# First-layer attention: the softmax division is done quad by quad between later units, with sums and reciprocals laid out by tokens

## What is computed

```python
q, k, v = xn @ Wq.T + bq, xn @ Wk.T + bk, xn @ Wv.T + bv     # 16 heads of 8
p = softmax(q @ k.T / sqrt(8))                                # 512 x 512 per head
out = ((p @ v) * head_mask) @ Wo.T + bo
```

## Time and profile before

| | us |
|---|---|
| median of 3 runs | 4028.96 (4026.98 to 4035.01) |
| the profiled execution | 4031.42 |
| its span, first to last instruction | 4030.1 |
| TensorE busy (share of the span) | 3097.7 (77%) |
| VectorE busy | 2581.5 (64%) |
| ScalarE busy | 2028.4 (50%) |
| GpSimd busy | 1557.2 (39%) |
| mean granted TensorE clock | 0.84 of full |
| first scores of attending in the first-layer attention, to its end | 118.2 to 672.95 |

### The profile page before, as it was taken

One profiled execution on the slowest core, in us unless ns is written; L12 is line 12 of the kernel. 1 busy time (PEld: TensorE's weight loads), 2 busy tenths in 40 slices (PEclk: granted clock), 3 DMA queues, 4 the chain that ended last, 5 costly groups with the idle time before them and its releaser, 6 DMA issues.

```text
span 4030.1 us, 40714 instructions
## 1 busy us (share of the span) xinstructions
PE 3097.7 (77%) x14760; PEld 1359.4 (34%) x14850; DVE 2581.5 (64%) x2891; ACT 2028.4 (50%) x3628; POOL 1557.2 (39%) x938
## 2 busy tenths in 40 slices
PE   5788877975567777777775879777687888888876
PEld 2111212341222222232322644322234554554544
DVE  4676662439998888888787334577625655555563
ACT  1454453134456766766664211576435565555654
POOL 2211100113457667666657002244414443443432
PEclk7788897986778888887777979888698998999998
DMA  3221200021111221121111001001000000000000
GB/s 86 41 33 30 45 3 0 0 75 39 26 35 37 42 51 32 40 49 36 32 34 45 1 0 64 21 21 32 11 0 19 19 19 10 19 19 10 19 10 31
DMA packets 79733, 114.60 MB, mean 28 GB/s; under 512 B 16270, under 2 KB 49422, under 8 KB 78106
## 3 DMA queue, kind: packets, MB, share of 16 engines
q1 hardware_dynamic: 68268, 103.33, 10.7%
q0 software_dynamic: 11264, 8.66, 1.6%
HBM read 37.96 MB, written 17.33 MB: 14 GB/s over the span
## 4 chain that ended last, share of the span: by engine, by line
PE 49%; DVE 21%; ACT 16%; issue 7%; POOL 3%; DMA 2%; SPq 1%; POOLq 0%; DVEq 0%; ACTq 0%
DVE layer_mamba_state L1340 7%; PE psum L1112 3%; DVE psum L1328 3%; PE psum L2460 3%; ACT layer_mamba_decay L1266 3%; PE psum L1189 3%; PE psum L2491 3%; PE psum L779 2%; ACT layer_exps L792 2%; PE psum L236 2%; PE psum L248 2%; PE psum L2154 2%; PE psum L905 2%; PE psum L242 2%; PE psum L2544 2%
## 5 line engine op out<-in xcount | busy, mean ns | idle before, releaser
L1369 POOL TENSOR_TENSOR layer_mamba_state<-layer_mamba_state,layer_mamba_c 128x1024 f32<-128x1024 f32 x320 | 781.0, 2450 | 591.3 <-DVE layer_mamba_state L1340 585.1
L1340 DVE TENSOR_TENSOR_SCAN layer_mamba_state<-layer_mamba_decay,psum 128x1024 f32<-128x1024 f32 x320 | 731.4, 2286 | 43.7 <-ACT layer_mamba_decay L1266 11.5
L1189 PE MATMUL psum<-layer_mamba_state,two_to_one 128*64 128x512 f32 x1280 | 442.9, 784 | 124.1 <-DVE layer_mamba_x L1357 80.9
L1266 ACT ACTIVATE layer_mamba_decay<-layer_mamba_delta_wide,layer_weights 128x511 f32<-128x511 f32 x640 | 415.7, 711 | 76.1 <-DMA layer_mamba_delta_wide<-layer_mamba_delta 39.5
L1328 DVE TENSOR_TENSOR psum<-psum,layer_mamba_u_wide 128x1024 f32<-128x1024 f32 x320 | 393.3, 1229 | 62.0 <-PE psum L1147 26.0
L720 DVE TENSOR_REDUCE layer_peak<-psum 128x2 f32<-128x1024 f32 x256 | 306.6, 1218 | 112.7 <-PE psum L691 108.6
L792 ACT ACTIVATE layer_exps<-psum 128x1024 f32<-128x1024 f32 x256 | 250.8, 1029 | 222.6 <-PE psum L759 222.6
L2857 POOL TENSOR_TENSOR layer_p<-layer_p,layer_stats 128x512 f32<-128x512 f32 x128 | 133.2, 1041 | 299.0 <-DVE layer_stats L2780 298.8
L2651 ACT ACTIVATE layer_p<-psum,layer_stats 128x128 f32<-128x128 f32 x512 | 181.5, 369 | 130.1 <-DVE layer_stats L2773 129.6
L2844 POOL TENSOR_TENSOR layer_qk<-layer_qk,layer_v_between 128x1024 f32<-128x1024 f32 x64 | 150.5, 2351 | 216.1 <-DVE layer_v_between L2744 214.3
L1147 PE MATMUL psum<-layer_mamba_bc,layer_mamba_pick 96*64 96x512 bf16 x768 | 164.2, 455 | 87.5 <-DVE psum L1328 63.7
(11 more groups left out here) (349 smaller groups left out, 6185.8 us busy)
## 6 DMA issues: line engine op xcount, KB each, us to landing
layer_mamba_delta_wide<-layer_mamba_delta SPq DMA_DIRECT2D x160, 128.0 KB, 2.4
layer_mamba_u_wide<-layer_mamba_work SPq DMA_DIRECT2D x160, 128.0 KB, 2.4
layer_v_between<-layer_v SPq DMA_DIRECT2D x16, 512.0 KB, 4.3
qk_dram<-layer_qk_parts SPq DMA_DIRECT2D x16, 384.0 KB, 3.0
layer_q_rows<-qk_dram SPq DMA_DIRECT2D x96, 64.0 KB
layer_k_rows<-qk_dram SPq DMA_DIRECT2D x96, 64.0 KB
layer_v_between<-layer_v SPq DMA_DIRECT2D x16, 384.0 KB, 5.6
layer_weights<-weights_dram SPq DMA_DIRECT2D x1, 4147.0 KB, 12.2
```

The lines of the kernel that those rows point to most:

```text
L1189: e = pe.matmul(c.psum[j * HALF:(j + 1) * HALF, self.sum_banks[h], :], c.two_to_one[:, :], self.state[i % len(self.state)][:, j, :], start ...
L1266: e = act.activation(decay[:, j, 1:SEQ], self.delta_wide[h][:, j, 1:SEQ], ACT.Exp, scale=rates[:, rate:rate + 1])
L1340: dve.tensor_tensor_scan(state, decay, self.fill.rearrange("p j t -> p (j t)"), 0.0, ALU.mult, ALU.add).then_inc(self.scanned, 1)
L1369: pool.tensor_tensor(state, state, self.both(self.c_wide[turn % self.C_BUFFERS][:, :]), ALU.mult).then_inc(self.multiplied, 1)
```

## The change

The sums are made per quad. For each block of 128 tokens the quad's tile is the weight operand and 4 columns of `sum_rows` move, so that sums come out by tokens: 128 rows by 4 columns, for four blocks 128x16 in bank 7. The reciprocal is taken there, 128x16, into `inverse`. To spread it over the quad's rows, a column of `inverse`, broadcast to 32 columns, is the weight operand and the identity moves: 16 products of 128 columns, into four groups of 32 rows by four blocks. Scaling and output product are as before.

The steps of `divide(b)` now have written-out times 32b + 10.6, 12.6 (quad 0: sums, spread), 18.6, 20.6 (quad 1), 28.6, 30.6 (quad 2), 34.6, 36.6 (quad 3) and 38.6 (output), for VectorE 0.6 and for ScalarE 0.9 later. The steps of `project` have 0.3 (wq), 3.6 (wk) and 8.8 (values) from 32(b-2), where they had 0.3, 2.3 and 6.3; SP's stores are at 1.3 and 4.6 and its row loads at 5.6 and 6.6, where they were at 1.3, 3.3, 4.3 and 5.3. The first sequence's projection is moved ahead by two units.

```diff
+    PROJECT_AT = (0.3, 1.3, 3.6, 4.6, 5.6, 6.6, 8.8, 9.8)
+    DIVIDE_AT = (10.6, 12.6, 18.6, 20.6, 28.6, 30.6, 34.6, 36.6, 38.6)
...
-        self.sums = buf("sums", [HEADS0, SEQ])
+        self.inverse = buf("inverse", [P, 4 * BLOCKS])
...
-        play(self.run(self.act_project, self.act_maxima, self.act_attend, self.act_divide))
-        play(self.run(self.dve_project, self.dve_maxima, self.dve_attend, self.dve_divide))
+        play(self.run(self.act_project, self.act_maxima, self.act_attend, self.act_divide, 0.9))
+        play(self.run(self.dve_project, self.dve_maxima, self.dve_attend, self.dve_divide, 0.6))
...
         for b in range(SEQS):
-            runs += [paced(divide(b), UNITS0 * (b + 1) + 1), paced(attend(b), UNITS0 * b + 0.1),
-                     paced(maxima(b), UNITS0 * (b - 1) - self.LEAD + 0.2),
-                     paced(project(b), (opening - 8, opening)[b] if b < 2 else UNITS0 * (b - 2) + 0.3)]
+            at = UNITS0 * (b - 2) if b > 1 else opening - 10 * (1 - b)
+            runs += [timed(project(b), [at + t for t in self.PROJECT_AT]), paced(maxima(b), UNITS0 * (b - 1) - self.LEAD + 0.2),
+                     paced(attend(b), UNITS0 * b + 0.1), timed(divide(b), [UNITS0 * b + t + after for t in self.DIVIDE_AT])]
...
     def pe_divide(self, b):
-        hold.wait_ge(self.heads_kept, QUADS0 * (b + 1))
-        c.wait_bank(7)
         for g in range(QUADS0):
-            m = pe.matmul(c.psum[0:HEADS0, 7, :], w["sum_rows"][:, g * HEADS0:(g + 1) * HEADS0], self.heads[g][:, :],
-                          start=g == 0, stop=g == QUADS0 - 1)
-        m.then_inc(self.sums_made, 1)
-        c.bank_read[7] = self.sums_inverted, b + 1
-        yield
-        for g in range(QUADS0):
-            hold.wait_ge(self.sums_inverted, b + 1)
+            n, first = QUADS0 * b + g + 1, g * HEADS0 + 4 * g
+            hold.wait_ge(self.heads_kept, n)
             c.wait_bank(7)
-            pe.matmul(bank, w["head_rows"][0:HEADS0, g * P:(g + 1) * P], self.sums[:, :], start=True, stop=True).then_inc(
-                self.sums_spread, 1)
-            c.bank_read[7] = self.heads_normed, QUADS0 * b + g + 1
+            for k in range(BLOCKS):
+                m = pe.matmul(bank[:, 4 * k:4 * k + 4], self.heads[g][:, k * P:(k + 1) * P], w["sum_rows"][:, first:first + 4],
+                              start=True, stop=True)
+            m.then_inc(self.sums_made, 1)
+            c.bank_read[7] = self.sums_inverted, n
+            yield
+            hold.wait_ge(self.sums_inverted, n)
+            c.wait_bank(7)
+            for k in range(BLOCKS):
+                for j in range(4):
+                    m = pe.matmul(c.psum[32 * j:32 * j + 32, 7, k * P:(k + 1) * P],
+                                  self.inverse[:, 4 * k + j:4 * k + j + 1].broadcast_to([P, 32]), c.ident[:, :],
+                                  start=True, stop=True)
+            m.then_inc(self.sums_spread, 1)
+            c.bank_read[7] = self.heads_normed, n
             yield
...
     def dve_divide(self, b):
-        hold.wait_ge(self.sums_made, b + 1)
-        hold.wait_ge(self.sums_spread, QUADS0 * b)
-        dve.reciprocal(self.sums[:, :], c.psum[0:HEADS0, 7, :]).then_inc(self.sums_inverted, 1)
-        yield
-        hold.wait_ge(self.out_made, b)
         for g in range(QUADS0):
-            hold.wait_ge(self.sums_spread, QUADS0 * b + g + 1)
+            n = QUADS0 * b + g + 1
+            hold.wait_ge(self.sums_made, n)
+            hold.wait_ge(self.sums_spread, n - 1)
+            dve.reciprocal(self.inverse[:, :], c.psum[:, 7, 0:4 * BLOCKS]).then_inc(self.sums_inverted, 1)
+            yield
+            hold.wait_ge(self.out_made, b)
+            hold.wait_ge(self.sums_spread, n)
```

More of the change, by code:

```diff
@@ L567, in nothing, with run @@
         return blank(0)
-    def run(self, project, maxima, attend, divide):
+    def run(self, project, maxima, attend, divide, after=0.0):
         runs, opening = [], -UNITS0 - self.LEAD
         for b in range(SEQS):
-            runs += [paced(divide(b), UNITS0 * (b + 1) + 1), paced(attend(b), UNITS0 * b + 0.1),
-                     paced(maxima(b), UNITS0 * (b - 1) - self.LEAD + 0.2),
-                     paced(project(b), (opening - 8, opening)[b] if b < 2 else UNITS0 * (b - 2) + 0.3)]
+            at = UNITS0 * (b - 2) if b > 1 else opening - 10 * (1 - b)
+            runs += [timed(project(b), [at + t for t in self.PROJECT_AT]), paced(maxima(b), UNITS0 * (b - 1) - self.LEAD + 0.2),
+                     paced(attend(b), UNITS0 * b + 0.1), timed(divide(b), [UNITS0 * b + t + after for t in self.DIVIDE_AT])]
         return merged(*runs)
@@ L836, in pe_divide @@
         c.bank_read[7] = self.attn_made, b + 1
-        yield
     def act_divide(self, b):
         c, act, hold = self.c, self.c.act, self.c.act_hold
-        yield from blank(1 + QUADS0)
+        yield from blank(2 * QUADS0)
         hold.wait_ge(self.out_made, b + 1)
         act.activation(self.out[:, b, :], c.psum[:, 7, :], ACT.Identity, bias=self.w["bo"]).then_inc(self.attn_made, 1)
-        yield
     def dve_divide(self, b):
         c, dve, hold = self.c, self.c.dve, self.c.dve_hold
-        hold.wait_ge(self.sums_made, b + 1)
-        hold.wait_ge(self.sums_spread, QUADS0 * b)
-        dve.reciprocal(self.sums[:, :], c.psum[0:HEADS0, 7, :]).then_inc(self.sums_inverted, 1)
-        yield
-        hold.wait_ge(self.out_made, b)
-        for g in range(QUADS0):
-            hold.wait_ge(self.sums_spread, QUADS0 * b + g + 1)
+        for g in range(QUADS0):
+            n = QUADS0 * b + g + 1
[5 more added lines that the diff above has]
+            hold.wait_ge(self.sums_spread, n)
             dve.scalar_tensor_tensor(self.normed[g][:, :], self.heads[g][:, :], self.w["mask_rows"][:, g:g + 1],
@@ L2911, in layer0_pieces @@
     sum_rows = np.zeros((P, QUADS0, HEADS0), np.float32)
-    head_rows = np.zeros((HEADS0, QUADS0, P), np.float32)
     for head in range(HEADS0):
@@ L2915, in layer0_pieces @@
         sum_rows[32 * j + DIM0, g, head] = 1.0
-        head_rows[head, g, 32 * j:32 * j + 32] = 1.0
     return {
@@ L2922, in layer0_pieces @@
         "mask_rows": np.repeat(i["L0_attn_head_mask"].reshape(QUADS0, 4), 32, axis=1).T,
-        "sum_rows": sum_rows.reshape(P, -1), "head_rows": head_rows.reshape(HEADS0, -1),
+        "sum_rows": sum_rows.reshape(P, -1),
     }, {
```

## The result

The changed kernel takes 3912.47 us (median of 4 runs, 3907.57 to 3920.47) against 4031.11 (4 runs, 4026.98 to 4035.01): ratio 0.9712, 95% interval 0.9698 to 0.9726. It is 119 us faster; 124 were forecast. The profiled execution took 3907.57, that of before 4031.42.

A forecast was written before the change was run, and what follows sets the result against it. Around the division no engine is full; they wait for each other at clock 0.69. Five periods of 71.6 us become 55.2 (-82); with +4, -12.6, -17, -16.2 that is -124, to 3908, or 3905 on the median's footing; range 3872 to 3950.

The forecast's parts named there:

- A boundary without low clock: Between sequences: with the division's boundary gone, turns and load take 46.1 us at full clock, before inserts.
- the low clock stays: Rival, chance 0.12: 5 us at half clock stay at each boundary, +15, 3920 us.
- Slack of 0.83 us in an even place: Behind a turn's first peak scores, 0.83 us of an insert is hidden; behind the second, the odd place, nothing.
- wk: Projection product at 3.6, an odd place: 1.15 us plus 0.35 for the last quad's reciprocal, together 1.5.
- The quads' sums: Sums take 1.2 us; shown: quad 3 0.35, quad 1 0.9, quad 0 1.55, the latter two behind their copy.
- The first two turns: Start of a period: wq shows 0.3 us and quad 3's sums at 2.6 show 0.35.
- The spread: Spreading a quad's inverses, 32 records: 1.2 us, near the weighing, of which 0.35 shows; three times, 1.05.
- the rival of the weight loads: Chance 0.12: loads in the open make a spread 0.9 us longer in 25 places, +23, 3928 us.
- VectorE's queue: Rival, chance 0.13: reciprocal and scaling ahead of the odd reduction hold TensorE's scores; period 62 us, total 3947.
- First sequence: Gains nothing, takes in quads 0 and 1 and the worse place of wk: +4.0 us.
- The eighth: Last sequence, ScalarE paces: 30.8 us of steps plus 2.5, 1.9 and 1.8 make 37.0, against 54.01.
- The tail: After the eighth, the last quad's division alone: 10 us against 26.25, output product 3.7 to 5 by the clock.

The follow-up runs named there:

- the last version: Changed kernel with the output product split into four quads' parts, every bank 7 product two units from the next, wk at 2.3: 3894.11 us, ratio 0.9666.
- the one with 16 columns inverted: Changed kernel's times with sums along the free dimension, the 4x512 reciprocal cut to its first 16 columns: 3920.2 us.
- the head by head order: Changed kernel with each spread's 16 products ordered so that four in a row go to the same group of 32 output rows: 3947.67 us.
- the 3.33 us reciprocal: Changed kernel's order, but sums and reciprocals along the free dimension, a reciprocal of 4x512 per quad: 4044.28 us, ratio 1.0036 to the kernel before.
- the layout alone: Kernel before with sums and reciprocals by tokens, all 16 heads at once at the boundary, in the old order: 3981.54 us, ratio 0.9875.

## Why the prediction was right

The forecast was 3905, the result 3912.5, inside the range and nearest to the case forecast. The stage gained 127.0 where the sum had 124, but part of this closeness is errors that cancel: the five periods, which I priced at 82 us, gave 86.8, and the other stretches 40 instead of 42. The changed kernel's profile is also the fastest of its four runs, 5 us below their median. By its steps:

- **A boundary without low clock.** Right, and the main thing. The five periods have clock 1.00. The rival "the low clock stays" is wrong for this kernel, but it was nearer than I thought: of the other kernels with short reciprocals, only the last version and the one with 16 columns inverted keep 1.00 in all five.
- **Slack of 0.83 us in an even place.** Right: spread 0.25 (forecast 0.35), values 0.35 (0.55), output 2.88 (2.9). Doubling the spread showed that it is used up.
- **wk** showed 1.08, not 1.5: the odd place has no cover, as said, but TensorE never waited for the reciprocal, only the load of its weights did. VectorE had done it at 227.85, 0.05 before wk.
- **The quads' sums.** Quad 0's wait for the copy is 0.66, with 0.96 shown (1.55), quad 1's, at 255.45, 0.38 with 0.69 shown (0.9). I had put a second copy's length, 0.7, for the value additions. They run from 240.54 to 241.41 and push back the reduction that the copy at 242.46 stands behind; against quad 1 this costs 0.28, not 0.7.
- **The first two turns**, wq and quad 3's sums, were too cheap at 0.65. The inserts above sum to 6.7 (three spreads among them), and 54.25 less 46.1 is 8.15, so 1.4 is left for them. The row at 226.03 names a part: the scores wait 0.94 for an exponential, where an undisturbed turn has 0.69, and this exponential stands in ScalarE's queue behind wq's bias step of 0.69, which I had costed at nothing. That is some 0.3 of the 0.8 that were missing. For the rest I have only an argument: no weighing stands in the first turn of a sequence, so an insert there finds less to hide behind than the 0.83 of a full turn.
- **The spread** took 1.01, where 1.2 was forecast. That it is near the weighing and not near single records was the choice that mattered most, and the head by head order shows how near the other side was: the rival of the weight loads gave 2.1, a mere change of loop order 2.39. (That rival's 0.13 us for a load pass doesn't follow from 0.16 for two; at 0.08 it would have stood at some 3920 instead of 3928.)
- **VectorE's queue.** The rival did not happen here: in the third sequence VectorE still idles 8.6 us before its 32 reductions, with 45.08 us busy (45.4 forecast). But with the 3.33 us reciprocal a chain through VectorE's queue does form, and costs more than the rival's 62: 74.3 to 75.9.
- **First sequence.** +4.0 forecast, +0.2 measured. The forecast was 3.8 too high: I added the inserts and took the clock as unchanged, but it was 0.90 before and is 0.97 after. By these two numbers that is some 3 of the 3.8 us, an estimate. Nothing shows that the change did it: the last version above has 0.91 there. So this term is as much luck as working.
- **The eighth**, 41.5 instead of 37.0, is the largest error. From the first exponential to the last, ScalarE is busy 31.6 us and idles 8.4 between its 33 steps; 0.4 ahead of them and the last weighing, 1.1 more, I had left out. I had 30.8 and 6.2. The output product alone holds up ScalarE for 2.93, not 1.9, since the next exponential's scores are behind it.
- **The seventh** took 53.41 for 52.2. Its clock is 0.97, and 1.2 us is within what that costs (1.6 us in the periods above); with the reciprocal of 16 columns, at 1.00, it takes 51.5.
- **The tail**: 11.3 for 10. The sequence of steps is right (sums, 0.26 reciprocal, spread, scaling, output), and its output product took 5.50, above the 3.7 to 5 that I gave it, since it runs at the low clock (0.70 in the tail), behind three waits of 0.84, 0.35 and 0.87 us.

## What to carry to other kernels

An engine's share of busy time doesn't tell whether a long instruction fits on it. Before interleaving a chain, take the longest instruction in it and ask which buffer it holds; here, 3.3 us in one bank turned a gain of 119 us into a loss of 15. Measure the slack of each place in the loop, one number from a timeline, and cut long inserts to it: four pieces in places with slack cost 1.2 us where one piece in such a place cost 2.88. And order small products so that neighbours fall into different groups of the array.

## What the runs showed of the hardware

- Thirty-two fp32 records of 128 columns with 32 weight loads take 1.08 us when four groups of 32 columns alternate, and 2.46 when they don't.
- A reciprocal of 4x512 takes 3.33 us, one of 16x512 3.35, one of 128x64 0.56 (the layout alone), one of 128x16 0.25 and one of 4x16 0.24: the time goes by elements along the free dimension, and the number of partitions makes no difference among these.
- Stretches at 1.2 GHz that cost a period 1.6 us or 3.2 us appear behind the start of a sequence in some orders and not in others, and differ between two executions of the same order (three periods of 56.2, or four of 54.7). In those two TensorE's last idle time ahead of such a stretch is the 0.94 us for the exponential, and the changed kernel has that wait as well and no such stretch in its five periods. An order that keeps 1.00 in one profile may not keep it in all.
